# A selective scan on four engines: one more of sixteen steps takes its input product from Pool, and TensorE drops one broadcast of B

## The reference

```python
u = _silu(causal depthwise conv of width 4 over the first half of x @ in_w.T)
delta = softplus(xdbl[..., :dt_rank] @ dt_w.T + dt_b)      # xdbl = u @ xproj_w.T
Bm, Cm = xdbl[..., dt_rank:dt_rank + 16], xdbl[..., dt_rank + 16:]
dA  = exp(einsum('bld,dn->bldn', delta, A))
dBu = einsum('bld,bln,bld->bldn', delta, Bm, u)
h_t = dA_t * h_{t-1} + dBu_t                               # scan over the tokens
y_t = einsum('bdn,bn->bd', h_t, C_t);  y = (y + u * D) * silu(res);  out = y @ out_w.T
```

## Time and profile before

| | us |
|---|---|
| median of 3 runs | 19913.28 |
| fastest and slowest of them | 19899.77, 19913.79 |
| the profiled execution | 19903.3 |
| its span, first to last instruction | 19901.5 |
| VectorE busy (DVE) | 18394.5, 92% |
| Pool busy | 16700.9, 84% |
| TensorE matmul busy (PE) | 13325.4, 67% |
| ScalarE busy (ACT) | 11270.3, 57% |
| mean granted TensorE clock | 0.776 |

### The profile page before, as it was taken

How to read it: one execution, slowest core, us unless ns; L and a number is a source line. 1 busy time by engine, 2 the same in 40 slices (tenths; PEclk the granted TensorE clock), 3 DMA queues, 4 the chain that set the end, 5 groups by cost and what they waited for, 6 DMA issues and landing times. The chain is left out here.

```text
span 19901.5 us, 149974 instructions
## 1 busy us (share of the span) xinstructions
PE 13325.4 (67%) x46814; PEld 4847.9 (24%) x46814; DVE 18394.5 (92%) x11898; ACT 11270.3 (57%) x12399; POOL 16700.9 (84%) x7161
## 2 busy tenths in 40 slices
PE   4776666666666666666666666666666668888885
PEld 2221111111111111111111111111111134444444
DVE  5889999999999999999999999999999979999996
ACT  1115666656665666566666666666656646666663
POOL 3878888888888888888888888888888869999991
PEclk8997777777777777777777777777777779999997
DMA  3325555555555555555455555555555511111113
GB/s 123 103 95 134 133 130 130 134 134 131 128 133 133 135 129 130 134 134 130 130 133 135 129 131 135 133 130 129 134 134 131 127 50 29 29 32 32 32 28 140
DMA packets 616206, 2249.36 MB, mean 113 GB/s; under 512 B 74881, under 2 KB 92147, under 8 KB 591091
## 3 DMA queue, kind: packets, MB, share of 16 engines
q1 hardware_dynamic: 610146, 2232.63, 43.1%
q10 hardware_dynamic: 5265, 7.14, 0.1%
HBM read 990.77 MB, written 174.96 MB: 59 GB/s over the span
## 5 line engine op out<-in xcount | busy, mean ns | idle before, releaser
L1324 POOL TENSOR_TENSOR h<-h,c_bc 128x1024 f32<-128x1024 f32 x4096 | 9619.3, 2359 | 1884.9 <-DVE h L1280 1884.7
L1280 DVE TENSOR_TENSOR_SCAN h<-da,state,px 128x1024 f32<-128x1024 f32 x3328 | 7811.2, 2347 | 273.4 <-PE py L1004 155.5
L1151 ACT ACTIVATE da<-d_bc,a_neg 128x1024 f32<-128x1024 f32 x3328 | 3787.0, 1145 | 3405.8 <-DVE h L1280 3384.6
L990 PE MATMUL px<-cf,bsel 32*128 32x512 f32 x4096 | 2036.5, 1088 | 3864.6 <-DVE h L1280 3864.6
L1274 DVE TENSOR_TENSOR px<-px,du_bc 128x1024 f32<-128x1024 f32 x3328 | 4099.4, 1232 | 332.4 <-PE px L990 87.1
L1910 POOL TENSOR_TENSOR acc<-acc,ta 128x1024 f32<-128x1024 f32 (+1 forms) x1040 | 2426.1, 2341 | 394.8 <-DVE acc L1810 288.6
L1004 PE MATMUL py<-h,ysel 128*32 128x512 f32 x16384 | 2357.4, 700 | 26.0 <-POOL h L1324 24.5
L1810 DVE SCALAR_TENSOR_TENSOR p_c<-zb,w_dw,p_c 128x1024 f32<-128x1024 f32 (+1 forms) x1560 | 1987.0, 1274 | 43.7 <-PE p_c L1582 11.2
L1316 POOL TENSOR_TENSOR xs<-du_bc,b_bc 128x1024 f32<-128x1024 f32 x768 | 1809.5, 2356 | 0.0
L1280 DVE TENSOR_TENSOR_SCAN h<-px,state,xs 128x1024 f32<-128x1024 f32 x768 | 1743.1, 2326 | 0.0
L990 PEld LDWEIGHTS px<-cf,bsel 32*128 32x128 f32 x4096 | 496.1, 291 | 4995.5 <-DVE h L1280 2934.6
(11 more groups left out here) (219 smaller groups left out, 18991.2 us busy)
## 6 DMA issues: line engine op xcount, KB each, us to landing
d_bc<-delta SPq DMA_DIRECT2D x1024, 512.0 KB, 8.5
du_bc<-du SPq DMA_DIRECT2D x1024, 512.0 KB, 8.3
c_bc<-c_rows_dram SPq DMA_DIRECT2D x1024, 512.0 KB, 4.7
b_bc<-c_rows_dram SPq DMA_DIRECT2D x256, 512.0 KB, 8.1
hx<-x_dram SPq DMA_DIRECT2D x252, 256.5 KB, 5.6
st_x<-in_x_dram SPq DMA_DIRECT2D x32, 1024.0 KB, 4.9
ax<-in_x_dram SPq DMA_DIRECT2D x64, 512.0 KB, 3.5
xr<-x_dram SPq DMA_DIRECT2D x64, 512.0 KB, 6.1
```

What stands on the lines that cost most here:

```text
L990: last = nc.tensor.matmul(px[(t.par + q + q // 2) % 2][:, cut], bsel[rows, q, :], cf[rows, cut], start=True, stop=True)
L1151: nc.scalar.activation(out[:, :], d_bc[:, n % J, :], ACT.Exp, scale=a_neg[t.l][:, n:n + 1]).then_inc(da_done, 1)
L1280: nc.vector.tensor_tensor_scan(h[:, n % 8, PAD:T + PAD], a[:, :], x[:, :], state[:, 2 * t.l + t.b, n:n + 1], ALU.mult, ALU.add).then_inc(s ...
L1324: nc.gpsimd.tensor_tensor(out=h[:, n % 8, 0:T], in0=h[:, n % 8, PAD:T + PAD], in1=c_bc[q % 2][:, :], op=ALU.mult).then_inc(m2_done, 1)
```

## The change

Step 11 becomes the fourth step whose product Pool makes and whose decay lies in PSUM. TensorE no longer makes B of the third group. Pool makes the product of step 11 behind step 5. ScalarE's order of decays changes, with that of step 11 last, after scan 9. On TensorE the second y sum, `add_y(t, 1)`, stands in front of B of the fourth group instead of behind it; that B keeps its wait for scan 10, and which of the two PSUM tiles it goes to stays the same. VectorE's product of step 12 still waits for it. One more tile `xs` is taken.

```diff
-    POOL_X = (8, 9, 10)
+    POOL_X = (8, 9, 10, 11)
...
-        POOL_X_AT = {0: 0, 2: 1, 3: 2}
-
-        DECAYS = (0, 1, 2, 3, 4, 5, 6, 7, 11, 12, 8, 13, 9, 10, 14, 15)
+        POOL_X_AT = {0: 0, 2: 1, 3: 2, 5: 3}
+
+        DECAYS = (0, 1, 2, 3, 4, 5, 6, 7, 12, 13, 8, 14, 9, 10, 15, 11)
...
-                    pe.wait_ge(scanned, t.nth((None, 2, 9, 10)[q], N))
+                    pe.wait_ge(scanned, t.nth((None, 2, None, 10)[q], N))
...
-                    last = nc.tensor.matmul(px[(t.par + q + q // 2) % 2][:, cut], bsel[rows, q, :], cf[rows, cut], start=True, stop=True)
+                    last = nc.tensor.matmul(px[(t.par + q // 3 + q) % 2][:, cut], bsel[rows, q, :], cf[rows, cut], start=True, stop=True)
...
-                spread_b(t, 2)
+                add_y(t, 1)
                 spread_b(t, 3)
-                add_y(t, 1)
...
-                decay(t, 11)
+                decay(t, 12)
                 keep_state(t, 0)
...
-                decay(t, 12)
+                decay(t, 13)
                 decay(t, 8)
-                decay(t, 13)
+                decay(t, 14)
                 decay(t, 9)
                 decay(t, 10)
-                decay(t, 14)
+                decay(t, 15)
+                decay(t, 11)
                 if before:
                     back_z(before)
                 keep_state(t, 1)
-                decay(t, 15)
...
-                       11: (far, far), **{n: (near, far) for n in range(12, 15)}, 15: (near, near)}
+                       **{n: (near, far) for n in range(12, 15)}, 15: (near, near)}
...
-                        if n in (0, 4, 11, 12):
-                            dve.wait_ge(b_ps, t.nth(q, Q))
+                        if j == 0:
+                            dve.wait_ge(b_ps, t.nth(min(q, Q - 2), Q - 1))
```

## The result

The changed kernel takes 19,587.8 us (median), against 19,910.4 us before: a ratio of 0.9838, interval 0.9824 to 0.9853, 1.6% faster.

What follows compares the result with a forecast made beforehand. VectorE, busy 92% of the span, was taken to bound the kernel. 2.12 us removed less 1.26 us new wait gave 220 us; less 25 us for du, 195 us: 19,715 us, range 19,600 to 19,830 us.

Steps and rivals of the forecast that it cites:

- What the change removes: On VectorE, step 11's product and step 12's y-sum wait go: 2.12 us a task, 543 us in 256 tasks.
- What it adds on Pool: One more product behind step 5, 2.32 us, of which 1.07 us reaches step 7; Pool is not the bound.
- T: The one scan-layer task read instruction by instruction; forecast wait of step 12's product for B there: 1.19 us.
- output task: The one task in four that also writes output; Pool has no gap there, forecast wait for B 1.46 us.
- The moved y sum: the new wait: Step 12's product waits for a chain of Pool step 7, y sum and B: 1.26 us a task in the mean.
- B takes 2.08 us: Last TensorE term before step 12's product: B of the fourth group, its length taken from the profile before.
- rival named "clock": TensorE back at 2.4 GHz by the time of B: 19,440 us, or up to 19,650 us if in part; chance 0.06.
- SyncE's queue: Broadcasts for the next task start later behind Pool's step 7, so du lands late: 0.1 us a task, 25 us.
- The forecast's own sign of being wrong: VectorE's waits for du passing 100 us would show the forecast wrong, towards slower.
- Moves that cost nothing: ScalarE's later decay 11 and state copy, and TensorE's variance product, delay nothing; cover of 1.1 us on ScalarE.
- uncovered-product rival: Pool reaches step 6 without idle in every task, so the new product isn't covered: 19,925 us, chance 0.06.
- the slower one: Du landings crowd to 9.5 us, so the next task's products wait 1.4 us: 20,041 us, chance 0.07.

Runs made afterwards that it cites:

- e4: Changed kernel with Pool's product du of the next task behind step 7 instead of behind step 6: 19,382.5 us, ratio 0.9736.
- e3: Changed kernel with the next task's three first delta broadcasts issued ahead of the fourth group's C broadcast: 19,481.9 us, ratio 0.9785.
- e1: Changed kernel with B of the fourth group back in front of the second y sum: 19,905.8 us, ratio 1.0000.
- e6: Kernel before with only the second y sum moved, in front of B of the third and fourth groups: 20,227.2 us, ratio 1.0163.
- e2: Changed kernel with three pairs of zero-weight matmuls in TensorE's idle stretch ahead of the second y sum: 19,558.5 us, ratio 0.9824.
- e5: Changed kernel with e3's broadcast order and four pairs of zero-weight matmuls ahead of the second y sum: 19,421.4 us, ratio 0.9757.

## Why the prediction was right and wrong, step by step

| term, us in 256 tasks | forecast | measured |
|---|---|---|
| gain without the new waits | 543 | 526 (before less e4, both of whose new waits are gone) |
| new wait for B | 323 | 99 by time (e3 less e4), 145 as listed |
| new waits for du | 25 | 106 by time (changed kernel less e3), 110 as listed |
| net | 195 | 323 |

The measured column splits one difference by way of e3 and e4, so that 526 - 99 - 106 = 321 us (323 us by the medians of the result) adds up by its making and proves nothing; the listed waits are the check on it. They are some 50 us more than the times. Most of that is a gap of some 0.1 us that these products have in front of them also where they wait for nothing (0.104 us at the median for step 12 in e4) and that a listed wait includes: 388 more waits make an estimated 40 us.

**What the change removes: right.** 526 us against 543 us. That this depends on the moved y sum was not a term of the forecast, but e1 and e6 show it: neither half has the gain alone.

**What it adds on Pool: right.** In T the new product, step 6, du and step 7 end 9.2 us behind step 5, forecast 9.28 us; Pool is not the bound. Behind scan 8's start, step 7 ends 4.50 us later in the mean of all tasks, forecast 4.54 us in T and 4.81 us in the output task.

**"The moved y sum: the new wait": the step that failed.** The chain is the one named, and e1 and e4 show it from both ends. Its last term was mis-sized: "B takes 2.08 us". In T it took 1.13 us, since the clock was back at 1.00 by then, and in the mean of all tasks 1.51 us. The idle time in front of the product of step 12 came out at 0.60 us in that mean, where 1.26 us were forecast; 0.57 of the 0.66 us between them is this term. I had dated the clock's rise from the start of the burst, the run of matmuls that follows TensorE's idle stretch: in the earlier trace rows the burst starts at 8022.34 and the clock is at 0.50 to 8028 at least. But two B's open that burst, and its y sum starts only at 8026.59; the clock is mostly up in the window from 8028. In the changed T the y sum opens the burst at 7878.46, and the clock is up from 7882, 3.5 us later. Over all tasks of the kernel before the rise came 6.2 to 9.6 us behind the burst's start, but 1.9 to 5.3 us behind the y sum's. Dated so, B, some 3.6 us behind the y sum's start, lies among the rises: fast in some tasks and slow in others, as it came out. The output task is one of the slow ones: 7.5 us behind the y sum's start, at 7942, the clock is still at 0.50. The output task's wait is also shorter than forecast at the same B, 0.86 against 1.46 us, because scan 8 starts (7930.21) only 4.2 us ahead of the y sum (7934.43), not 4.9 us (8074.63 and 8079.52). VectorE had been held up in that task by du, in the timeline

```profile
7902.61 1.23 DVE L1273 TENSOR_TENSOR px<-px,du_bc 128x1024 f32<-128x1024 f32 x1 [0.77 <-DMA du_bc<-du]
```

while Pool has no idle there to be held up in. e3 bears this out: without the waits for du, Pool's step 7 ends 4.79 us behind scan 8's start in the mean of the output tasks, against 4.58 us in the changed kernel. A wait for du thus takes the place of a part of the wait for B; the two terms are not independent, as my sum had them.

So the rival named "clock" came true in a part of the tasks, and the time lies in its 19,440 to 19,650 us; 0.06 was too little for it. A page of the Trainium skill (TensorE: Matmul & The Clock Gate, Part 1) has it that activity releases the throttle. I had drawn from it that B would run fast, and had held the row of before against that, though this row showed a burst that opened with other matmuls. In T, B ran fast (1.13 us), in the task behind it not (2.08 us).

**SyncE's queue: the right place, the wrong size.** 0.1 us a task was chosen since there were "only 4 waits" before; it was 0.43 us. The forecast's own sign of being wrong, waits for du above 100 us, came true. The step that failed is the lead. It was worked out for du of block 1 alone, but the products of blocks 0, 1 and 2 all waited, in 73, 76 and 46 tasks (idle over 0.15 us, counted from the trace). And it shrank by more than 1.93 us: from issue to its product, block 1 had 11.0 us at the median of all tasks before and 8.4 us after, 2.6 us less. The task became 1.25 us shorter and not 0.86 us, which is 0.4 us of the 0.7 us by which the lead shrank too much; the rest is not taken apart. Landings took longer too, by 0.6 us at the median, the view of the earlier trace rows after the change:

```profile
DMA to landing us min/median/max: 6.7/8.9/14.6
```

The errors by the times: 224 us too much for B, 81 us too little for du, 17 us too much for the gross gain; together, to a microsecond, the 127 us by which the time was missed.

**Moves that cost nothing: right.** No wait for a decay or a state copy stands in VectorE's list. The uncovered-product rival and the slower one did not come about.

## What to carry to other kernels

Where two queues meet in a chain (Pool's step, y sum, B, product), work taken off an engine may be worth nothing until its feeder is reordered too, so test each half: here one half alone gave nothing and the other cost 1.6%. After a change, ask which single event both new waits hang on; moving one Pool instruction behind it was worth another 1.0%. Price a short matmul group at both clocks, and don't carry the moment of the clock's rise over from a burst whose order the change rewrites.

## What the runs showed of the hardware

The same 4 matmuls of B take 2.08 us at a granted clock of 0.50 and 1.13 us at 1.00; the y sum's 16 take 3.62 to 3.64 us and 1.93 us. TensorE's idle stretch ahead of the burst was over 7.1 us in every task of the kernels before and after, and the burst began at 0.50 each time. With two B's at its head (before) the clock rose 6.2 to 9.6 us behind the burst's start, with one (e1) 3.9 to 7.3 us; behind the start of the y sum it was 1.9 to 5.3 us in both. With the y sum at its head (after) it was 2.7 to 9.5 us. So the distance from the burst's start depends on what the burst opens with; what spreads it from task to task is open. Matmuls with zero weights in the idle stretch raised the mean granted clock from 0.794 to 0.832 (changed kernel to e2) and from 0.797 to 0.837 (e3 to e5).
